# A selective-scan kernel with three decay banks: ScalarE's side work moved between units

## The reference

```
z   = layernorm(x)                           # the gate
xin = in_proj_w @ ctx                        # 512 channels x 512 steps
u   = silu(causal_conv4(xin) + conv_b)
dt_lo, B, C = split(x_proj_w @ u, [16, 16, 16])
delta = softplus(dt_proj_w @ dt_lo + dt_proj_b)
state[e, n] = state[e, n] * exp(delta[e] * A[e, n]) + delta[e] * u[e] * B[n]   # per step
y[e] = sum_n state[e, n] * C[n] + D[e] * u[e]
x    = x + y * silu(z)
```

## Time and profile before

| what | us |
|---|---|
| median of 3 runs | 1292.38 (1291.54 to 1293.58) |
| the profiled execution | 1297.83 |
| its span | 1296.1 |
| VectorE (DVE) busy | 762.3 |
| GpSimd (POOL) busy | 640.3 |
| ScalarE (ACT) busy | 524.1 |
| TensorE (PE) busy | 1129.2 |

### The profile page before, as it was taken

How to read it: one execution, slowest core, us unless ns; L and a number is a source line. 1 busy time by engine, 2 the same in 40 slices (tenths; PEclk the granted TensorE clock), 3 DMA queues, 4 the chain that set the end, 5 groups by cost and what they waited for, 6 DMA issues and landing times.

```text
span 1296.1 us, 19383 instructions
## 1 busy us (share of the span) xinstructions
PE 1129.2 (87%) x4940; PEld 843.6 (65%) x4940; DVE 762.3 (59%) x823; ACT 524.1 (40%) x706; POOL 640.3 (49%) x465
## 2 busy tenths in 40 slices
PE   5677977887878778837999999999999999999994
PEld 2344554455446545636888888888888888888883
DVE  5898899879997998657324353531532434324321
ACT  6955765665566564213223142321421323213210
POOL 0799899988998799304122232222321223212221
PEclk9686597777787666656999999999999999999997
DMA  7422243422332233055314353421531434215310
GB/s 225 139 90 92 81 122 88 167 73 82 107 143 77 82 91 128 0 215 207 99 33 169 107 178 110 165 101 49 178 98 40 170 107 178 99 42 174 106 46 20
DMA packets 65444, 145.08 MB, mean 112 GB/s; under 512 B 8654, under 2 KB 11214, under 8 KB 65408
## 3 DMA queue, kind: packets, MB, share of 16 engines
q1 hardware_dynamic: 56368, 116.34, 26.9%
q0 software_dynamic: 9040, 28.32, 6.7%
HBM read 320.53 MB, written 18.35 MB: 261 GB/s over the span
## 4 chain that ended last, share of the span: by engine, by line
PE 52%; DVE 2%; issue 0%; ACT 0%; POOL 0%; ACTq 0%; DVEq 0%; POOLq 0%
PE hp L1507 11%; PE hp L1506 11%; PE hp L1505 11%; PE yp L1505 5%; PE yp L1507 5%; PE yp L1506 5%; PE tp L1546 2%; PE xp L1499 1%; PE yp L1551 0%; DVE R L1343 0%; DVE S_tok L1339 0%; DVE S_w L1334 0%; DVE S_w L1447 0%; DVE S_w L1445 0%; DVE xT_lo L1402 0%
## 5 line engine op out<-in xcount | busy, mean ns | idle before, releaser
L284 POOL TENSOR_TENSOR ring<-du,bB 128x1024 f32<-128x1024 f32 x128 | 298.6, 2356 | 35.2 <-DVE du L654 34.9
L588 DVE TENSOR_TENSOR_SCAN ring<-dA,ring 128x512 f32<-128x512 f32 x256 | 296.0, 1205 | 14.9 <-ACT dA L368 9.3
L368 ACT ACTIVATE dA<-delta,Acol 128x512 f32<-128x512 f32 x256 | 172.2, 687 | 174.3 <-DVE ring L588 171.6
L1505 PE MATMUL hp<-w_hi,xT_hi 128*128 128x512 f32 x592 | 236.7, 400 | 2.1 <-DVE xT_lo L1402 2.1
L1507 PE MATMUL hp<-w_hi,xT_lo 128*128 128x512 f32 x592 | 236.3, 399 | 0.0
L1506 PE MATMUL hp<-w_lo,xT_hi 128*128 128x512 f32 x592 | 234.4, 396 | 0.0
L753 PEld LDWEIGHTS yT<-ident,ring 128*128 128x128 f32 x1024 | 152.6, 178 | 97.9 <-issue 77.8
L733 PE MATMUL Cb<-xdbl,ident 48*128 48x512 f32 x176 | 130.0, 827 | 85.1 <-DVE ring L594 84.8
L753 PE MATMUL yT<-ident,ring 128*128 128x128 f32 x1024 | 179.7, 341 | 9.0 <-POOL ring L293 9.0
L1144 POOL COPY out_index<-out_tab 128x1 uint32 x37 | 6.7, 181 | 357.4 <-DVE work L1409 357.4
L1423 DVE TENSOR_TENSOR work<-hp,work 128x512 f32<-128x512 f32 x74 | 51.1, 691 | 224.3 <-PE hp L1507 221.2
(11 more groups left out here) (202 smaller groups left out, 1413.1 us busy)
## 6 DMA issues: line engine op xcount, KB each, us to landing
stage<-in_L_ffn_w_kernel_dram SPq DMA_DIRECT2D x160, 1024.0 KB
stage<-in_L_ffn_wo_kernel_dram SPq DMA_DIRECT2D x78, 1024.0 KB
bB<-bcs SPq DMA_DIRECT2D x64, 512.0 KB, 3.7
bC<-bcs SPq DMA_DIRECT2D x40, 256.0 KB, 4.4
xall<-in_x_dram SPq DMA_DIRECT2D x1, 4096.0 KB, 13.9
xln_dram<-xlnb SPq DMA_DIRECT2D x4, 1024.0 KB, 6.8
out_dram<-xall SPq DMA_DIRECT2D x4, 1024.0 KB, 8.9
ctx_rows<-in_ctx_dram SPq DMA_DIRECT2D x4, 512.0 KB, 5.5
```

Of the source, the lines that this page charges most:

```text
L284: g_.tensor_tensor(ring[:, q % RING, :].rearrange("p (e l) -> p e l", e=2), dub(b, h * 2 * L, 2 * L).rearrange("p (e l) -> p e l", e=2), B ...
L368: a_.activation(dA[r % SB][:, :], db(b, eb * L, L), ACT.Exp, scale=Acol[:, eb, n:n + 1]).then_inc(exp_done, 1)
L588: v_.tensor_tensor_scan(o, dA[r % SB][:, :], o, 0.0, ALU.mult, ALU.add).then_inc(scan_done, 1)
L1505: t_.matmul(bank[:, :], a_hi[:, k, :], b_hi[:, b, :], start=(start and k == ks[0]), stop=False)
```

## The change

On ScalarE:

- `soft` is cut into `soft_exp` and `soft_plus`. For the second half they follow units 2 and 3 (both were behind 2); for the next batch's first half both follow unit 25 (was 24), and `dt_half` stays behind 24.
- `soft_log(b, 1)` follows unit 8 in batches 1 to 3 (was 5).
- `guess_2` first loads the set that has Ln and Exp.
- `xln` follows unit 12 (was 13).
- `silu_z(b + 1)` follows unit 16; `silu_u(b + 1)` stays behind 18. Both were behind 18, u first.

On GpSimd `rstd_2` stands at s = 12 (was 14), `add_ln(b, 1)` at 13 (was 11) and `times_u(b, 1)` at 15 (was 13). On VectorE `loss(b + 1, 0)` follows unit 26 (was 25).

```diff
--- before.py
+++ after.py
@@ -333,12 +333,12 @@
                         add_y(b - 1, 1)
                     if s == 9:
                         sub_loss(b, 1)
-                    if s == 11:
+                    if s == 12 and b > 0:
+                        rstd_2(b - 1)
+                    if s == 13:
                         add_ln(b, 1)
-                    if s == 13:
+                    if s == 15:
                         times_u(b, 1)
-                    if s == 14 and b > 0:
-                        rstd_2(b - 1)
                     if s == 24:
                         add_y(b, 0)
                     if s == 28 and b + 1 < NB:
@@ -442,10 +442,13 @@
                     act.wait_ge(freed[k % 2], nth(k))
                 act.sem_inc(relu_done, 1)
 
-            def soft(b, i):
+            def soft_exp(b, i):
                 g = 2 * b + i
                 act.wait_ge(abs_done, g + 1)
                 a_.activation(spy[:, :], spy[:, :], ACT.Exp, scale=-1.0).then_inc(soft_y, 1)
+
+            def soft_plus(b, i):
+                g = 2 * b + i
                 act.wait_ge(soft_y, g + 1)
                 if g > 0:
                     act.wait_ge(delta_ready, g)
@@ -467,6 +470,7 @@
                 guess(rs1, mv1, rstd1_guess, 1)
 
             def guess_2(b):
+                a_.preload_act_table_set("natural_log_exp_and_others")
                 act.wait_ge(stats2, b + 1)
                 guess(rs2, mv2, guess2, 3 + 2 * b)
 
@@ -507,7 +511,8 @@
             last.then_inc(diag_ok, 1)
             x_dbl(0)
             dt_abs_first()
-            soft(0, 0)
+            soft_exp(0, 0)
+            soft_plus(0, 0)
             dt_relu_first()
             soft_log(0, 0)
             a_.preload_act_table(ACT.Exp)
@@ -518,17 +523,19 @@
                 for s in range(UPB):
                     exp_dA(b * UPB + s)
                     if s == 2:
-                        soft(b, 1)
+                        soft_exp(b, 1)
+                    if s == 3:
+                        soft_plus(b, 1)
                     if s == 3 and nxt:
                         ctx_T(b + 1)
                     if s == 3 and not rest:
                         guess_1()
-                    if s == 5:
-                        soft_log(b, 1)
                     if s == 6 and rest:
                         zs_T(b, (0, 1))
                     if s == 8 and rest:
                         zs_T(b, (2, 3))
+                    if s == (8 if rest else 5):
+                        soft_log(b, 1)
                     if s == 6 and not rest:
                         silu_z(b)
                     if s == 7 and not rest:
@@ -543,14 +550,15 @@
                     if s == 11 and rest and nxt:
                         tap(b + 1, 0)
                         tap(b + 1, 1)
-                    if s == 13 and rest:
+                    if s == 12 and rest:
                         xln(b - 1)
                     if s == 15 and nxt:
                         tap(b + 1, 2)
                         tap(b + 1, 3)
+                    if s == 16 and nxt:
+                        silu_z(b + 1)
                     if s == 18 and nxt:
                         silu_u(b + 1)
-                        silu_z(b + 1)
                     if s == 19 and rest:
                         gate_T(b - 1, 0)
                         gate_T(b - 1, 1)
@@ -558,7 +566,9 @@
                         x_dbl(b + 1)
                     if s == 24 and nxt:
                         dt_half(b + 1, 0)
-                        soft(b + 1, 0)
+                    if s == 25 and nxt:
+                        soft_exp(b + 1, 0)
+                        soft_plus(b + 1, 0)
                     if s == 27 and nxt:
                         soft_log(b + 1, 0)
                     if s == 28 and nxt:
@@ -678,7 +688,7 @@
                         conv(b + 1, (2, 3))
                     if s == 18:
                         drain_y(b, 0)
-                    if s == 25 and nxt:
+                    if s == 26 and nxt:
                         loss(b + 1, 0)
                 if rest and nxt:
                     logit_copy(b - 1)
```

## The result

| kernel | median us | runs |
|---|---|---|
| before | 1291.54 | 5 (1283.68 to 1293.58) |
| changed | 1298.82 | 5 (1298.46 to 1301.56) |

The ratio is 1.0070, with a 95% interval of 1.0036 to 1.0103: the change makes the kernel slower, by 7.3 us in the medians.

A forecast was written before the change was run, and what follows sets the result against it. VectorE (114 of 129 us busy) and GpSimd (123) were both judged close to full, neither fully. Terms gave -3.0 from the profiled 1297.83 (1294.8) and +1.6 from the median 1292.38 (1294.0); forecast 1294.4, range 1288.3 to 1301.

The forecast's parts named there:

- the sum from the profile: All batches' terms added to the profiled execution of 1297.83 us: -3.0, so 1294.8.
- the second sum: Terms from the median of 1292.38, assuming the median run lacked the 7.64 us loss: +1.6, so 1294.0.
- rival (c): GpSimd's 2.75 paid at all boundaries and xln gain swallowed, or lower TensorE clock, or costly table switches: 1297.5; chance 0.15.
- Loss of the next batch one unit later: Loss behind unit 26 ends 2.75 us later in three batches, delaying GpSimd's queue; bounds 0 to 10.1.
- Batch 0 to 1: First boundary: GpSimd's delay makes VectorE wait 0.6 us for unit 0 and delays TensorE's fill for unit 1; +1.7.
- Newton group: Earlier rstd_2 and xln remove VectorE's waits of 2.61 and 0.18 in batch 1, 0.60 and 0.19 in batch 3: -2.79, -0.79.
- rival (a): The gains arrive and VectorE's wait at the boundary hides the later loss: 1285.5 to 1290; chance 0.22.
- silu apart: Silus behind units 16 and 18: waits go, but VectorE next waits for TensorE; gain taken as 0, other end -2.07.
- softplus, soft_log: Moving soft_log costs 0; waits of 0.48, 0.48, 0.38 at unit 25 go, 1.09 and 1.08 stay.
- one of my signs of being wrong: VectorE's wait for ScalarE, 9.3 us before, was to fall to 2 to 3; above 6 would mean wrong.
- The loss beside GpSimd: Loss starts only when a GpSimd operation ends: batch 1 +1.1; batch 3 -5.87, or -1.25 against a loss of 3.02.
- Rival (b): GpSimd passes VectorE over once at batch 1's loss, +4.7 to +9.4: 1299 to 1304; chance 0.16.

The follow-up runs named there:

- loss25: Changed kernel with only the loss of the next batch's first half put back behind unit 25; 1286.77 us, ratio to before 0.9972.
- b_loss26: Kernel before with one edit, the loss of the next batch's first half behind unit 26; 1300.79 us, ratio 1.0048.
- b_gate_loss26: Kernel before with GpSimd's unit-8 multiply waiting for VectorE's second-half loss, and the next batch's loss behind unit 26; 1306.44 us, ratio 1.0101.
- b_silu: Kernel before with only silu of the gate moved behind unit 16, silu of u behind 18; 1296.86 us, ratio 1.0016.
- b_split: Kernel before with only the softplus in two pieces, loss staying behind unit 25; 1294.40 us, ratio 1.0008.
- b_newton: Kernel before with only rstd_2, add_ln, times_u, xln, soft_log and the table set moved as in the change; 1297.26 us, ratio 1.0027.
- best: loss25 with both pieces of the softplus behind unit 2 in batch 0; 1296.32 us, ratio to before 1.0003.
- spread: best with logits of batches 0 and 1 made behind units 1 and 2 of the batch after the next, copied behind unit 3; 1289.27 us, ratio 0.9937.
- the gate: One added GpSimd wait: its unit-8 multiply waits for VectorE's second-half loss; on the kernel before 1291.78 us, on best 1283.08, on the changed kernel 1299.13.

## Why the prediction was right in its sign and short in its size

- *How much of it was luck.* By pieces of the profile the forecast was, for batches 0 to 3, +1.7, +0.35, +1.6 and -6.7, and 0 for the set-up: -3.0. Measured: +2.0, +4.5, +7.5, -13.2 and +2.6, +3.4 in all. So the sum from the profile had the wrong sign; the forecast's sign came from the second sum, +1.6 from the median, which rests on a guess about the 7.64. The two together gave 2.0 us, less than the 2.6 that a measurement was said to tell from nothing. The range held the result by its width. Nearest was rival (c), 1297.5, with 0.15: of its conditions the lower clock through the logits came, and the table switches did not show.
- *Loss of the next batch one unit later.* The chain was right: GpSimd's wait, its queue, the logits. GpSimd's wait was to be near 5.4 and is 5.48 and 5.46; 14 to 17 in all, and is 16.4; the wait for the logits 24 to 29, and is 27.7. The term was mis-sized. I let the string behind it on TensorE keep the length that it had in the profile of before, and gave the lower clock to rival (c). Behind the wait of 2.4 the same instructions take 6.3 us longer than in loss25, twice; against the profiled execution of before, which had part of this already, they take 0.8 and 4.0 longer. I wrote +1.7, +2.0 and +1.6, 5.3 us in all; b_loss26 and loss25 put it at 7 to 12 in all, b_gate_loss26 at 15. That the wait causes the lower clock is not shown.
- *Batch 0 to 1*, +1.7, measured +2.0 by the batch's width. That is near by chance, for the waits in it are others. VectorE waits 2.66 for unit 0 where 0.6 was reckoned; this is the later loss, for b_loss26 has 2.64 and loss25 none. The fill for unit 1 was 2.71 late where about 1.1 was reckoned; this is not the loss alone, for loss25 has 2.39 and b_silu 2.16, with none in before, and why is open. I had also overlooked ScalarE in the first units of batch 0, where its side work stands without a gap: the copy behind unit 3 delays it to units 4 and 7, which b_split shows by itself (0.85 and 4.07, in place of 0.62 and 3.52 for GpSimd).
- *Newton group*, -2.79 and -0.79: the waits went, as b_newton shows. There 2.81 reached the end of batch 1 and was lost in batch 2. "All gains before it are spent" was the right sentence for the changed kernel; in rival (a) I gave them too much.
- *silu apart*, 0: right, no wait shows. The Trainium skill's 2.66 us for a switch (ScalarE: Activation LUTs, What ACT_TABLE_LOAD costs) would have had a wait of 1.4 in each batch; b_silu has none.
- *softplus, soft_log*: the waits at unit 25 went, and those at unit 29, which I held at 1.09, are 1.41: the loss, and with it the logarithm and the table load, come later than I reckoned. That is 4.2 in three batches; another 4.9 are the waits at units 4 and 7 of batch 0. VectorE's waits for ScalarE are therefore 9.2 and not 2 to 3, and above 6 was one of my signs of being wrong: the path through ScalarE was misjudged, though the time did not hang on it.
- *The loss beside GpSimd.* Batch 1: 3.12 in the place of the reckoned 2.85. Batch 3: 2.50, reckoned 1.8, was 7.64. That the 7.64 was chance and not in most runs was a guess; of the fourteen profiled executions four (before, loss25, best, spread) have a loss of 7.6 to 12.3, and of the five with the gate none has one above 5.43. But batch 3 was 13.2 shorter, of which this is 5.1; the last logits at the full clock (the wait 3.20, was 7.23) are another 4, and most of the rest is shorter waits for ScalarE (0.8) and for TensorE's fills and transposes (about 2.8). Rival (b) had GpSimd pass VectorE over where the request falls 1.7 us or more before the end of an operation. That does not decide it: in the changed kernel the loss at 183.60 asks 2.0 before an end and gets in there, and in loss25 the one at 177.97 asks 2.0 before an end and gets in (3.10) while the one at 429.48 asks 1.9 before an end and does not (9.96).
- *Set-up*: 2.56 us of the 3.7 between the profiles are the first products at another clock. The same eight products of 128 x 512, behind the same wait of 0.73, take 3.67 from 9.29 on before and 5.98 from 9.53 on after. The first scans of the profiled kernels begin at 38.7 to 39.0 or at 40.8 to 41.6, whichever the kernel.

What stays open: what lowers the clock at the logits where TensorE has not waited, why GpSimd lets the loss in at its first end in one case and not in another, and what the other edits give under the later loss. The batch-0 edit of best is not told apart from nothing.

## What to carry to other kernels

When a wait lands on TensorE ahead of a string of small products, read at which clock the string ran in your profile, price it at the lower one as well, and look for an execution of each kind before you believe one profile. On two nearly full engines, an instruction moved by one slot on the first costs the whole queue behind its reader on the second; read what the reader's engine has in line up to the next point where all meet. Where the runs of one kernel fall into groups, find the event behind them before comparing medians: here one wait on GpSimd went with the highest runs gone.

## What the runs showed of the hardware

- 32 products of 128 x 8 take 3.64 or 6.83 us by the clock. With the sixteen transposes, the fill and the eight transposes ahead of them it is 7.9 us in a stretch granted 1.00 (loss25) and 14.2 in one granted 0.50 (the changed kernel, 288.5 to 302.8). The low level stood there behind a wait of 2.42 us, and also, at 0.54, in an execution of before with no wait in the stretch.
- A VectorE instruction with both inputs in SBUF (1.20 us alone) can be passed over at two to four ends of GpSimd instructions of 2.34 in a row (7.64 in before, 9.96 in loss25, 9.94 in best and 12.29 in spread); in all four it got in when GpSimd stopped to wait for VectorE. At other times it got in at the first end (1.71, 3.02, 3.12 us).
- A table load runs ahead of the wait of the instruction that needs it: in batch 1 of the changed kernel the load runs from 271.88 to 273.16, ahead of the loss at 273.27, and the logarithm starts at 274.53 behind a wait of 1.37 for the loss, so this load costs nothing.
